# Cross network tower: three of seven first-layer products as three passes on split operands made on Pool

## The reference

```
e  = stack of tbl_f[ids[:, f]]                       # 512 x 39 x 16
Xi = e
for W, b in (W0, b0), (W1, b1), (W2, b2):             # 128 outputs each
    Xi = einsum('hjk,bjd,bkd->bhd', W, e, Xi) + b     # Xi: 39, then 128, then 128 rows
    res.append(Xi.sum(axis=2))
h = concat(res + dense_ctx)                           # 384 + 16
h = relu(h @ W_top1 + b_top1); h = relu(h @ W_top2 + b_top2); y = h @ W_top3
```

## Time and profile before

| | |
|---|---|
| median of 3 runs | 681.0 us (680.91 to 682.17) |
| the profiled execution's own time | 682.09 us |
| its span, first to last instruction | 680.3 us, mean granted TensorE clock 0.995 |
| PE matmul busy | 646.9 us, 2662 instructions |
| DVE busy | 572.9 us |
| ACT busy | 561.3 us |
| POOL busy | 359.6 us |
| first-layer products (L958) | 114.5 us of PE, 224 records, two for each product |

### The profile page before, as it was taken

One profiled execution on the slowest core, in us unless ns is written; L12 is line 12 of the kernel. 1 busy time (PEld: TensorE's weight loads), 2 busy tenths in 40 slices (PEclk: granted clock), 3 DMA queues, 4 the chain that ended last, 5 costly groups with the idle time before them and its releaser, 6 DMA issues.

```text
span 680.3 us, 11318 instructions
## 1 busy us (share of the span) xinstructions
PE 646.9 (95%) x2662; PEld 483.9 (71%) x2662; DVE 572.9 (84%) x894; ACT 561.3 (83%) x1941; POOL 359.6 (53%) x394
## 2 busy tenths in 40 slices
PE   2789989999999999999999999999999999989898
PEld 2656767777777777777777777777777777767584
DVE  2548878989898998989898989898989899999870
ACT  2339879989898989988888989898989888899762
POOL 7554884664747474838384756557474323142700
PEclk9898999999999999999999999999999999999999
DMA  8215631405051414141322314050504040200000
GB/s 285 22 16 117 157 48 25 97 13 109 10 112 10 109 13 106 17 99 23 78 44 54 69 32 91 14 105 9 113 8 111 8 106 3 84 1 1 1 1 0
DMA packets 67522, 39.52 MB, mean 58 GB/s; under 512 B 58790, under 2 KB 61862, under 8 KB 65348
## 3 DMA queue, kind: packets, MB, share of 16 engines
q1 hardware_dynamic: 60463, 37.71, 24.9%
q0 software_dynamic: 5120, 1.29, 2.2%
q10 hardware_dynamic: 1904, 0.15, 0.2%
HBM read 32.80 MB, written 2.40 MB: 52 GB/s over the span
## 4 chain that ended last, share of the span: by engine, by line
PE 79%; DVE 9%; ACT 5%; issue 5%; DMA 1%; another core or an unknown queue 1%; DVEq 0%; ACTq 0%; SPq 0%
PE yb L992 18%; PE yb L996 17%; PE yb L993 17%; PE p L958 12%; PE pq L969 5%; DVE acc L816 3%; ACT yb L634 3%; DVE x L822 2%; PE yb L910 2%; DVE yb L800 1%; DVE x1l L874 1%; PE yb L1099 1%; PE pq L923 1%; DMA gram<-in_L_rec_W_dram 1%; PE p L1071 1%
## 5 line engine op out<-in xcount | busy, mean ns | idle before, releaser
L634 ACT ACTIVATE yb<-yb,x0t 128x128 f32<-128x128 f32 x1728 | 467.1, 366 | 58.3 <-PE yb L996 52.1
L816 DVE TENSOR_TENSOR acc<-acc,yb 128x512 f32<-128x512 f32 (+1 forms) x512 | 323.5, 668 | 34.8 <-ACT yb L634 33.8
L992 PE MATMUL yb<-w1h,x1h 128*128 128x512 f32 (+1 forms) x640 | 309.0, 483 | 8.9 <-DVE acc L816 7.6
L996 PE MATMUL yb<-w1h,x1l 128*128 128x512 f32 (+1 forms) x640 | 248.1, 388 | 0.0
L993 PE MATMUL yb<-w1l,x1h 128*128 128x512 f32 (+1 forms) x640 | 247.7, 387 | 0.0
L427 POOL DMA_INDIRECT emb<-in_table_dram,idx x160 | 152.8, 955 | 48.6 <-issue 40.5
L485 POOL TENSOR_TENSOR late<-late,x0r 117x512 f32<-117x512 f32 (+1 forms) x105 | 132.6, 1296 | 82.1 <-DMA late<-x_scratch 81.8
L992 PEld LDWEIGHTS yb<-w1h,x1h 128*128 128x128 f32 x640 | 120.6, 188 | 65.9 <-DVE acc L816 28.0
L993 PEld LDWEIGHTS yb<-w1l,x1h 128*128 128x128 f32 x640 | 121.0, 189 | 45.9 <-issue 24.8
L996 PEld LDWEIGHTS yb<-w1h,x1l 128*128 128x128 f32 x640 | 120.5, 188 | 25.2 <-DVE x1l L771 0.4
L474 POOL TENSOR_TENSOR bdiag<-mask,x0t 128x312 f32<-128x312 f32 x64 | 45.5, 711 | 145.2 <-PE pq L969 142.0
(11 more groups left out here) (108 smaller groups left out, 325.0 us busy)
## 6 DMA issues: line engine op xcount, KB each, us to landing
late<-x_scratch SPq DMA_DIRECT2D x45, 312.0 KB
late<-x_scratch SPq DMA_DIRECT2D x30, 234.0 KB
emb<-in_table_dram,idx POOLq DMA_INDIRECT x160
gram<-in_L_rec_W_dram SPq DMA_DIRECT2D x1, 2496.0 KB
x_scratch<-x0r SPq DMA_DIRECT2D x15, 156.0 KB
late<-x_scratch SPq DMA_DIRECT2D x15, 156.0 KB
w2t<-in_L_rec_W_dram SPq DMA_DIRECT2D x1, 1280.0 KB
x0t<-embt SPq DMA_DIRECT2D x64, 20.0 KB
```

Source lines behind the costliest of these rows:

```text
L634: op = act.activation(part, part, ACT.Copy, scale=x0t[u][:, t, j:j + 1])
L816: dve.tensor_tensor(part, part, parts(y_bank(t, m), n), ALU.add).then_inc(summed, 1)
L992: pe.matmul(y[:, 0:w], hi, w1h[:, at:at + w], start=True, stop=False)
L996: pe.matmul(y[:, 0:w], lo, w1h[:, at:at + w], start=False, stop=True).then_inc(bank_ready, 1)
```

## The change

Chunks 4, 5 and 6 (`HALVED`) of groups 2 to 15 get another form. Pool writes three tensors for each in place of one: the product rounded to fp32r (`pair_h`), the product in fp32 in place (as before), and the difference of the two (`pair_l`, fp32r), with a wait for its own two results ahead of the difference. PE multiplies in three fp32r passes (high weights x high pairs, low weights x high pairs, high weights x low pairs) and waits for `pair_low` in place of `pairs_ready`. High and low parts of the three weight blocks are made once by Pool, ahead of its chunks for group 1. The buffers are the eight `spare` tiles, which the kernel before uses only in its last part. Groups 0 and 1, and chunks 0 to 3, stay as they were.

```diff
+HALVED = (4, 5, 6)
+HALF_RING = 3
...
+        pair_h, pair_l = spare[0:HALF_RING], spare[HALF_RING:2 * HALF_RING]
+        w0h, w0l = (spare[i][0:ROWS, 0:len(HALVED) * HID] for i in (6, 7))
...
@@ Pool, pair_chunk @@
+                if c not in HALVED or not at_least(g, 2):
+                    pool.tensor_tensor(pairs[0:rows, c, :], pairs[0:rows, c, :], x0r[0:rows, :],
+                                       ALU.mult).then_inc(pairs_ready, 1)
+                    return
+                k = HALVED.index(c)
+                r = k % HALF_RING
...
+                pool.tensor_tensor(pair_h[r][0:rows, :], pairs[0:rows, c, :], x0r[0:rows, :],
+                                   ALU.mult).then_inc(pair_high, 1)
                 pool.tensor_tensor(pairs[0:rows, c, :], pairs[0:rows, c, :], x0r[0:rows, :],
                                    ALU.mult).then_inc(pairs_ready, 1)
+                pool.wait_ge(pair_high, (g - 2) * len(HALVED) + k + 1)
+                pool.wait_ge(pairs_ready, g * CHUNKS + c + 1)
+                pool.tensor_tensor(pair_l[r][0:rows, :], pairs[0:rows, c, :], pair_h[r][0:rows, :].bitcast(F32),
+                                   ALU.subtract).then_inc(pair_low, 1)
...
+            pool.wait_ge(w_hi, W0_BANKS)
+            for rows, c0, c1 in ((ROWS, HALVED[0], CHUNKS - 1), (LAST_ROWS, CHUNKS - 1, CHUNKS)):
+                of = w0t[0:rows, c0:c1, :].rearrange("p c h -> p (c h)")
+                w = slice((c0 - HALVED[0]) * HID, (c1 - HALVED[0]) * HID)
+                pool.tensor_copy(w0h[0:rows, w], of).then_inc(w0_split, 1)
+                pool.wait_ge(w0_split, 1 if rows == ROWS else 3)
+                pool.tensor_tensor(w0l[0:rows, w], of, w0h[0:rows, w].bitcast(F32), ALU.subtract).then_inc(w0_split, 1)
             for c in range(EARLY):
                 pair_chunk(1, c)
...
@@ PE, layer0 @@
+                if c in HALVED and at_least(g, 2):
+                    k = HALVED.index(c)
+                    r = k % HALF_RING
+                    w = slice(k * HID, (k + 1) * HID)
+                    pe.wait_ge(pair_low, (g - 2) * len(HALVED) + k + 1)
+                    pe.matmul(p0[:, :], w0h[0:rows, w], pair_h[r][0:rows, :], start=False, stop=False)
+                    pe.matmul(p0[:, :], w0l[0:rows, w], pair_h[r][0:rows, :], start=False, stop=False)
+                    op = pe.matmul(p0[:, :], w0h[0:rows, w], pair_l[r][0:rows, :], start=False, stop=(c == CHUNKS - 1))
...
             period(0, 0, 2)
+            pe.wait_ge(w0_split, 4)
             period(1, 1, 2)
```

More of the change, by code:

```diff
@@ L251, in tower @@
         bias_ready = sem("bias_ready")
+        w0_split = sem("w0_split")
+        pair_high = sem("pair_high")
+        pair_low = sem("pair_low")
+        half_used = sem("half_used")
         h1_done = sem("h1_done")
@@ L484, in pair_chunk @@
                     pool.wait_ge(rolled_in[c // EARLY], g * (16 * REPS))
+                if c not in HALVED or not at_least(g, 2):
[4 more added lines that the diff above has]
+                r = k % HALF_RING
+                if c < EARLY:
+                    pool.wait_ge(l0_done, g)
+                if k >= HALF_RING:
+                    pool.wait_ge(half_used, (g - 2) * (len(HALVED) - HALF_RING) + k - HALF_RING + 1)
+                pool.tensor_tensor(pair_h[r][0:rows, :], pairs[0:rows, c, :], x0r[0:rows, :],
+                                   ALU.mult).then_inc(pair_high, 1)
                 pool.tensor_tensor(pairs[0:rows, c, :], pairs[0:rows, c, :], x0r[0:rows, :],
                                    ALU.mult).then_inc(pairs_ready, 1)
+                pool.wait_ge(pair_high, (g - 2) * len(HALVED) + k + 1)
+                pool.wait_ge(pairs_ready, g * CHUNKS + c + 1)
+                pool.tensor_tensor(pair_l[r][0:rows, :], pairs[0:rows, c, :], pair_h[r][0:rows, :].bitcast(F32),
+                                   ALU.subtract).then_inc(pair_low, 1)
             def period(g, u, after):
@@ L956, in layer0 @@
                 rows = ROWS if c < CHUNKS - 1 else LAST_ROWS
+                if c in HALVED and at_least(g, 2):
[6 more added lines that the diff above has]
+                    op = pe.matmul(p0[:, :], w0h[0:rows, w], pair_l[r][0:rows, :], start=False, stop=(c == CHUNKS - 1))
+                    if c == CHUNKS - 1:
+                        op.then_inc(l0_done, 1)
+                    elif k < len(HALVED) - HALF_RING:
+                        op.then_inc(half_used, 1)
+                    return
                 pe.wait_ge(pairs_ready, g * CHUNKS + c + 1)
```

## The result

The changed kernel takes **704.3 us** (703.4 to 706.9, 4 runs) beside 681.0 for the kernel before: ratio 1.035, interval 1.033 to 1.037. The forecast was 676.2, the range ended at 681.0. So it is wrong in its sign: 23 us slower, 28 away from the forecast.

A forecast was written before the change was run, and what follows sets the result against it. The chain runs mostly on PE through chunks 4 and 5, then on ACT and DVE, which hide chunk 6. 28 x 0.17 = 4.8 us less takes 681.0 to 676.2; range 673.4 to 681.0.

The forecast's parts named there:

- The gathers: POOL's last four gathers, issued later among the shifted-row loads, land at 380.3, 0.2 us ahead of ACT; costed at zero.
- rival C: Gathers land late at ACT's transposing, bank 2 of tile 0, in 12 periods: 688 or 705 us; chance 0.14.
- My price of a wait beyond 0.4 us: At ACT's transposing, a wait of more than 4.8 / 12 = 0.4 us a period turns the gain into a loss.
- Three passes: On PE, three fp32r passes per chunk cost 0.68 to 0.70 us in place of 0.86, saving 0.17.
- Which count: Chunks 4 and 5 on PE's path in 14 periods, 28 x 0.17 = 4.8 us; chunk 6 hidden, costed at nothing.
- rival A: Chunk 6 counts too: PE's whole saving, 42 x 0.17 = 7.1 us, time 673.9; chance 0.10.
- Rival B: ACT or DVE takes over in tile 3; only chunk 4's saving passes, 2.4 us, time 678.6; chance 0.12.
- Rival D: Gain spent on small things (late gathers, POOL's 84 new instructions disturbing DVE): within 1.4 us of 681.0; chance 0.09.
- POOL: POOL's block of chunks 4 to 6 takes 12.1 us for 3.8; 8 us to spare, so PE does not wait.
- The Trainium skill: Warm 512-column PE pass about 216 ns: new product 0.65 us, sum below 5.9; forecast went by the trace's 0.227.

The follow-up runs named there:

- after_g2404_again: The whole change with its last four gathers moved to tile 3 (2, 4, 0, 4), rerun on a chip that holds: 677.9 us beside 682.4, ratio 0.993.
- pe_only: PE's three passes alone against the kernel before; POOL makes one fp32r product per chunk, low part left out: 677.6 us beside 681.8, ratio 0.994.
- mixed45: Changed kernel with only chunks 4 and 5 in three passes and POOL's gathers taken apart among the block's instructions: 678.1 us beside 682.7, ratio 0.993.
- after45: Changed kernel with only chunks 4 and 5 in three passes, POOL's order unaltered, on the chip without a hold: 669.0 us beside 673.4, ratio 0.993.
- after_g2404: The whole change with its last four gathers moved to tile 3 (2, 4, 0, 4), on the chip without a hold: 669.8 us beside 673.4, ratio 0.995.
- pe_only6: Kernel before with PE's three passes for chunk 6 alone, low part of its pairs left out: 682.8 us beside 682.7, ratio 1.000.
- before_g262: Kernel before with gathers at (2, 6, 2, 0) instead of (2, 4, 4, 0), on the chip without a hold: 672.7 us beside 673.4, ratio 1.000.
- before_g280: Kernel before with gathers at (2, 8, 0, 0) instead of (2, 4, 4, 0), eight in one row in tile 1: 727.6 us, ratio 1.066.

## Why the prediction was wrong

**The step that failed is "The gathers".** It asked when the moved gathers would land, and costed them at zero or, in rival C, by ACT's wait at its transposing. It did not ask how they would stand on POOL: that two fours, held apart only by POOL's wait for PE, would close up to eight. Every number for it was there. The text itself took 5.6 us for a spread with four gathers and placed the tile 2 spread at 367.9, right behind. What I did not know is that a row of eight costs anything: it was put at nothing, and it costs 2.4 to 3.1 us in each of 12 periods. Yet the trace of before had a row of ten in its start-up, and the prediction did not ask whether PE's updates came on time; 14 of those up to 60 us did not.

**Rival C** gives 705 for its upper case, next to the 704.3 measured, and is wrong all the same. In the kernel after ACT waits 0.4 us in all for the landing, once. Where gathers do land late, in `after_g2404_again`, ACT waits 0.86 us in each of 12 periods, and the gain of 4.5 us is there. A period is only 0.07 us longer than in `pe_only`. My price of a wait beyond 0.4 us was therefore also wrong: the place has play that the rows of ACT did not show me. The landing took 5.1 us there (375.60 to 380.70), not the 7.8 of period 0.

**What held.**

- *Three passes* cost 0.23 + 0.23 + 0.23 in the chain, as forecast 0.68 to 0.70.
- *Which count*: 4.2 us in `pe_only`, 4.6 in `mixed45`, 4.5 in `after_g2404_again`, and 4.4 and 3.6 in `after45` and `after_g2404` on the other chip, for 4.8. A period became 0.30 us shorter (`pe_only`, `mixed45`), for 0.34. Chunk 6 brings nothing (`pe_only6`), so rival A falls. Rival B's gain was 2.4; the lower ends of the first three intervals are 2.6, 3.1 and 2.5, so it falls too, by little. Rival D's nothing is not what came either.
- *POOL*: the block went from 358.85 to 370.46, 11.6 us for 12.1 (in its sum 9 x 1.26 is 11.3 and not 11.4, which changes nothing). Chunk 4's low part was written by 362.75 and PE came for it at 373.96, 11 us later where I had said 8. PE never waits for `pair_low`, and POOL still waits for the loads ahead of chunk 0:

```profile
358.85 1.30 POOL L505 TENSOR_TENSOR spare<-late,x0r 117x512 fp32r<-117x512 f32 x1
...
361.46 1.30 POOL L511 TENSOR_TENSOR spare<-late,spare 117x512 fp32r<-117x512 f32 x1
...
369.21 1.29 POOL L511 TENSOR_TENSOR spare<-late,spare 78x512 fp32r<-78x512 f32 x1
...
389.18 2.53 POOL L496 TENSOR_TENSOR late<-late,x0r 117x512 f32<-117x512 f32 x2 [5.46 <-DMA late<-x_scratch]
```

- *The Trainium skill* ("TensorE: Matmul & The Clock Gate", "Back-to-back issue gap") would have made the new product 0.65 us and the gain 5.9, by its figure for an isolated pass. The chain has 0.69, and no run gained over 4.6.

**What stays open.** By which path a row of gathers delays PE's updates, and why only PE's; whether the recording of the trace has a part in it; where between four and six the limit lies; and what sets apart the chip that holds nothing. The change in its own form was not measured on that chip; `after45`, with its rows of eight, gained 4.4 us there. All that is said of chips without a hold rests on one chip.

## What to carry to other kernels

When a change delays one engine's queue, write down what then stands back to back on it, not only when its results are due: a wait that looks idle may be what paces a row of transfers. If consumers idle "for PE" while PE's records are dense, compare the time of the semaphore update with the end of the pass, and look at what POOL is doing. Break rows of indirect gathers into fours, or put a short piece of work between them, and time such a kernel on more than one chip.

## What the runs showed of the hardware that was not expected

- An unbroken row of eight indirect gathers, 1.25 us apart, delays the recorded semaphore updates of PE by up to 3.7 us in the stretch shown and lets them go in a burst 0.05 us apart, 1.2 us behind the last gather's instruction. The recorded updates of ACT, DVE and POOL are on time meanwhile.
- It grows with the row: 0 to 0.1 us a period for four, 0.9 for six, 3.4 to 4.7 for eight (the upper figures with a part of lower clock). At 1.57 us from start to start eight cost nothing, so what serves the gathers may need between 1.25 and 1.57 us for each (an estimate from the two pitches, not measured by itself).
- It depends on the chip: none in any row on one chip, where the kernel before took 673.4 us; on the others it took 681 to 683, and 8.4 us of difference are there by the time that a tenth of PE's matmuls have started, the stretch with the row of ten, a part of them by a granted clock of 0.94 for 1.00.
- On the chips that hold, 12% of the records of PE's updates are missing in the kernel before (604 of 687), mostly within 1.3 us behind the start of a gather; on the other chip none is (691 of 691 in `before_g262`).
- The granted clock can fall behind PE's idle time and add to its cost: PE was busy 1.28 us of the 3.4 ahead of 117.1 us in `before_g280`, which then ran at 0.5, 27 us in all up to 520 us, and PE's busy time was 14 us longer for the same products.
